# A two-attention transformer block with routed experts: weights handed over laid out, and the first copies of K sent ahead of Q

## The reference

```python
x = x + attn_a(layernorm(x))   # inside: layernorm, q/k/v with biases, 16 heads of 8,
                               # windows of 64 rows every 32, blended; wproj; residual;
                               # layernorm, MLP 128 -> 512 -> 128 with exact gelu
x = x + ffn(layernorm(x))      # router Wr (8 experts), top 2 of the softmax, renormalised;
                               # expert e: silu(x W1[e].T) W2[e].T
x = x + attn_b(layernorm(x))   # one head of 128, windows of 128 rows every 64, averaged
x = x + ffn(layernorm(x))      # the same experts again
```

## Time and profile before

| | |
|---|---|
| median of 3 runs | 584.41 us (582.85 to 586.38) |
| span of the profiled execution | 580.7 us |
| the profiled execution's own device time | not shown |
| PE busy | 483.9 us (83%) |
| DVE busy | 306.7 us (53%) |
| ACT busy | 243.7 us (42%) |
| POOL busy | 247.1 us (43%) |
| granted PE clock, mean | 0.891 |

### The profile page before, as it was taken

One profiled execution on the slowest core, in us unless ns is written; L12 is line 12 of the kernel. 1 busy time (PEld: TensorE's weight loads), 2 busy tenths in 40 slices (PEclk: granted clock), 3 DMA queues, 4 the chain that ended last, 5 costly groups with the idle time before them and its releaser, 6 DMA issues.

```text
span 580.7 us, 12462 instructions
## 1 busy us (share of the span) xinstructions
PE 483.9 (83%) x4005; PEld 383.5 (66%) x4027; DVE 306.7 (53%) x1012; ACT 243.7 (42%) x507; POOL 247.1 (43%) x229
## 2 busy tenths in 40 slices
PE   1879999999989999888799999907997499999960
PEld 0546776768666887585797787705777388787750
DVE  5676496858876898445740110055867743010116
ACT  7735566574547443604223232315764033232330
POOL 7143363335332655540547443520217536643450
PEclk9959899999989996968679999956999579999995
DMA  7882293985669183010022310040001222331007
GB/s 241 247 164 44 62 165 90 138 157 76 131 95 174 25 156 57 14 52 19 29 70 70 99 47 23 35 145 1 1 2 48 61 61 61 94 80 31 25 24 217
DMA packets 66593, 48.35 MB, mean 83 GB/s; under 512 B 7861, under 2 KB 60615, under 8 KB 66534
## 3 DMA queue, kind: packets, MB, share of 16 engines
q1 hardware_dynamic: 61430, 36.99, 31.0%
q0 software_dynamic: 5104, 10.57, 5.2%
HBM read 16.14 MB, written 27.59 MB: 75 GB/s over the span
## 4 chain that ended last, share of the span: by engine, by line
PE 67%; DVE 12%; issue 7%; SPq 5%; POOL 3%; DMA 3%; ACT 2%; DVEq 0%; POOLq 0%
PE PS L806 13%; PE PS L651 9%; PE PS L790 7%; PE PS L792 4%; SPq L303 4%; PE PS L638 3%; PE PS L791 3%; PE PS L613 3%; PE PS L701 3%; PE PS L554 2%; PE PS L661 2%; POOL XS L494 2%; PE PS L595 2%; PE PS L622 2%; PE PS L632 2%
## 5 line engine op out<-in xcount | busy, mean ns | idle before, releaser
L506 POOL DMA_INDIRECT YY<-W2R,ID x78 | 76.8, 985 | 84.0 <-ACT W2R L1263 65.4
L450 POOL TENSOR_TENSOR R<-NM,I64B 128x1024 bf16<-128x1024 f32 x32 | 61.6, 1924 | 109.1 <-DVE NM L1425 104.1
L1255 ACT ACTIVATE W2R<-PS 128x512 f32<-128x512 f32 x78 | 46.6, 597 | 121.2 <-PE PS L792 121.2
L806 PE MATMUL PS<-WB,W2R 128*128 x624 | 90.9, 291 | 0.1
L790 PE MATMUL PS<-QKM,WA 128*128 128x128 bf16 x312 | 73.2, 236 | 10.5 <-issue 4.3
L806 PEld LDWEIGHTS PS<-WB,W2R 128*128 128x128 f32 x624 | 78.1, 197 | 2.4 <-issue 0.3
L494 POOL DMA_INDIRECT XS<-W1R,SLOT x64 | 63.6, 994 | 37.0 <-DVE SLOT L1551 20.0
L1698 DVE COPY QKM<-PS 128x1024 bf16<-128x1024 bf16 (+1 forms) x20 | 13.5, 677 | 123.2 <-PE PS L769 123.2
L792 PE MATMUL PS<-QKM,WA 128*128 128x128 bf16 x312 | 73.2, 236 | 0.0
L791 PE MATMUL PS<-QKM,WA 128*128 128x128 bf16 x312 | 71.1, 229 | 0.0
L651 PEld LDWEIGHTS PS<-VB,PF 128*128 128x128 f32 x512 | 62.8, 201 | 8.6 <-issue 8.6
(11 more groups left out here) (207 smaller groups left out, 875.7 us busy)
## 6 DMA issues: line engine op xcount, KB each, us to landing
XS<-CST SPq DMA_DIRECT2D x30, 520.0 KB, 10.1
QKM<-XS SPq DMA_DIRECT2D x78, 65.0 KB
QKM<-QK SPq DMA_DIRECT2D x64, 72.0 KB, 2.1
QKM<-YY SPq DMA_DIRECT2D x16, 256.0 KB, 5.0
W2R<-in_W POOLq DMA_DIRECT2D x1, 2048.0 KB, 11.2
YY<-W2R,ID POOLq DMA_INDIRECT x78, 2.2
XS<-CST SPq DMA_DIRECT2D x2, 585.0 KB, 10.8
XS<-W1R,SLOT POOLq DMA_INDIRECT x64, 2.4
```

The costliest lines, as they stand in the source:

```text
L450: nc.gpsimd.tensor_tensor(R[:, u % 2], NM[:, u % 2].unsqueeze(2).to_broadcast([P, NH, WIN]), I64B[:].unsqueeze(1).to_broadcast([P, NH, WIN ...
L506: pool.indirect_dma_start(out=YY[f], out_offset=to, in_=YS[n % NY][:, i, :], in_offset=None, bounds_check=NPAIRS - 1, oob_is_err=False) \
L806: last = mm(o, HF[n % 3][:, k, :], WB[:, e, k, :].rearrange("p o c -> p (o c)"), start=k == 0, stop=k == KF - 1)
L1255: fn(HF[n % 3], PS[:, n % 3, :].rearrange("p (k s) -> p k s", k=KF), ACT.Silu).then_inc(s["f_hf"], 1)
```

## The change

The host hands the weights over laid out, and 8 loads take the place of 28 (and of POOL's 2): x of block 0, CST, EARLY (the small columns, Wr transposed, wq and wk; 139 KB), MID (the other small matrices and the MLP; 896 KB), three rows, x of blocks 1 to 3, W1 transposed (128 rows of 16 KB) and W2 transposed, which lands in WB itself (128 rows of 16 KB). All are on SP's queue. The transposes of W1, W2 and Wr, their waits and their copies out of PSUM are gone. What is left of W1's preparation is the bf16 split, now from SBUF: ACT copies expert t at the end of unit t (units 0 to 7), DVE subtracts expert t - 1 at the end of its work in unit t (units 1 to 8). WRT is a part of EARLY. HF and YS get a tile of their own (HYS).

`place` now sends the four K copies first, for every block and half, and Q and K have semaphores of their own: `scores` waits for K alone, `scores_t` for Q.

At the start POOL zeroes SELB instead of VB, and VB only after XZ of block 0 is done; DVE's 16 casts into SELB are spread, four each, between the variance steps and behind XZ. Waits of PE on the copies of transposed weights are replaced by waits on the copies of QK or QF that used the same PSUM bank.

The diff, cut ("..." marks what is left out):

```diff
+def laid_out(x):
+    column = lambda *names: [x[n].reshape(-1, P).T for n in names]
...
+    return {"x": x["x"], "early": np.concatenate(early, axis=1), "mid": np.concatenate(mid, axis=1),
+            "rows": np.concatenate([x[n] for n in ("bproj", "b2", "bo_b")])[None],
+            "W1t": x["W1"][::-1].transpose(2, 0, 1).reshape(P, NE * DFF),
+            "W2t": x["W2"][::-1].reshape(NE, D, KF, P).transpose(3, 0, 2, 1).reshape(P, NE * DFF)}
...
+            load(EARLY[:], a["early"], "ld_early")
+            load(MID[:], a["mid"], "ld_mid")
+            load(ROWS[:].rearrange("o r d -> o (r d)"), a["rows"], "ld_rows")
             load(X[:, TB:NT, :], xv[:, TB:NT, :], "ld_x_rest")
+            load(W1R[:], a["W1t"], "ld_w1")
+            load(WB[:].rearrange("p e k d -> p (e k d)"), a["W2t"], "ld_w2")
...
-                for m in range(2):
+                for m in (1, 0):
                     for i in range(4):
                         rows = slice(32 * i, 32 * i + 32)
-                        sp.dma_start(QKM[rows, m, half, i], QK[rows, m, half]).then_inc(s[f"a_m{half}"], 16)
+                        sp.dma_start(QKM[rows, m, half, i], QK[rows, m, half]).then_inc(s[f"a_{'qk'[m]}{half}"], 16)
...
-            nc.gpsimd.memset(VBF[:], 0.0).then_inc(s["pool_consts"], 1)
+            nc.gpsimd.memset(SELB[:], 0.0).then_inc(s["sel_zero"], 1)
...
             rstd(1, "a", 2)
-            nc.gpsimd.memset(SELB[:], 0.0).then_inc(s["sel_zero"], 1)
+            pool.wait_ge(s["a_xz"], TB)
+            nc.gpsimd.memset(VBF[:], 0.0).then_inc(s["pool_consts"], 1)
             pool.wait_ge(s["ld_const"], 16)
-            pool.dma_start(W2R[:], a["W2"].rearrange("e d f -> d e f")).then_inc(s["ld_w2"], 16)
-            pool.dma_start(WRN[:], a["Wr"]).then_inc(s["ld_router"], 16)
...
-                    pe.wait_ge(s[f"a_m{h}"], 16 * 8 * (b + 1))
+                    pe.wait_ge(s[f"a_k{h}"], 16 * 4 * (b + 1))
...
+                if t % 4 == 0:
+                    pe.wait_ge(s[f"a_q{h}"], 16 * 4 * (b + 1))
                 pe.wait_ge(s["a_r"], u + 1)
...
-            for e in range(NE):
-                pe.wait_ge(s["a_sel"], min(e, 3) + 1)
-                if e >= 4:
-                    pe.wait_ge(s["wt_lo"], e - 3)
-                transpose_weights(e, e % 4)
...
+            def weights_hi(e):
+                act.wait_ge(s["ld_w1"], 16)
+                fn(WA[:, 0, e, :], W1R[:, DFF * e:DFF * e + DFF], ACT.Copy).then_inc(s["wt_hi"], 1)
...
-                for e, bank in W2_STEPS.get((c, t), ()):
-                    weights_hi(NE + e, bank)
+                if c == 0:
+                    weights_hi(t)
...
+            def weights_lo(e):
+                dve.wait_ge(s["wt_hi"], e + 1)
+                hi, lo = (WA[:, c, e, :] for c in range(2))
+                v.tensor_tensor(lo, W1R[:, DFF * e:DFF * e + DFF], hi, ALU.subtract).then_inc(s["wt_lo"], 1)
...
+                if c == 0 and t >= 1:
+                    weights_lo(t - 1)
+                if c == 1 and t == 0:
+                    weights_lo(NE - 1)
...
             dve.wait_ge(s["ld_x"], 16)
             input_variance(0)
-            input_second_variance(0)
-            input_normalised(0)
             dve.wait_ge(s["ld_const"], 16)
             dve.wait_ge(s["sel_zero"], 1)
+            selectors(0)
+            input_second_variance(0)
+            selectors(1)
+            input_normalised(0)
+            selectors(2)
+            selectors(3)
             for m in range(2):
                 split_qk(0, m)
-            for e in range(NE):
-                weights_lo(e)
             input_variance(1)
```

More of the change, by code:

```diff
@@ L119, in constants @@
     return np.concatenate([c[n] for n in COLS], axis=1)
+EARLY_COLS, MID_COLS = {}, {}
+for _cols, _names in ((EARLY_COLS, (("cols_a", 6), ("cols_b", 3), ("b1", FA), ("bv", 1), ("Wr", NE), ("wq", D), ("wk", D))),
+                      (MID_COLS, (("wv", D), ("wproj", D), ("Wo_b", D), ("Wq_b", D), ("Wk_b", D), ("Wv_b", D),
+                                  ("w1", DA), ("w2", DA)))):
+    for _n, _w in _names:
+        _cols[_n] = (sum(w for _, w in _cols.values()), _w)
+NEARLY, NMID = (sum(w for _, w in c.values()) for c in (EARLY_COLS, MID_COLS))
+def laid_out(x):
+    column = lambda *names: [x[n].reshape(-1, P).T for n in names]
+    early = column("ln1_g", "ln1_b", "ln2_g", "ln2_b", "bq", "bk", "bq_b", "bk_b", "bv_b", "b1", "bv")
+    early += [x["Wr"].T, x["wq"], x["wk"]]
+    mid = [x[n] for n in ("wv", "wproj", "Wo_b", "Wq_b", "Wk_b", "Wv_b", "w1")]
+    mid += [x["w2"].reshape(FA, P, D).transpose(1, 0, 2).reshape(P, DA)]
+    return {"x": x["x"], "early": np.concatenate(early, axis=1), "mid": np.concatenate(mid, axis=1),
+            "rows": np.concatenate([x[n] for n in ("bproj", "b2", "bo_b")])[None],
+            "W1t": x["W1"][::-1].transpose(2, 0, 1).reshape(P, NE * DFF),
+            "W2t": x["W2"][::-1].reshape(NE, D, KF, P).transpose(3, 0, 2, 1).reshape(P, NE * DFF)}
 class Steps:
@@ L172, in program, with early, mid @@
         ident = cst("ident")
[L174 to L178, removed]
-        ROWS = sb("ROWS", [1, 3, D])
[L180 to L184, removed]
+        EARLY, MID, BQS = sb("EARLY", [P, NEARLY]), sb("MID", [P, NMID]), sb("BQS", [P, 1])
+        def early(name):
+            o, w = EARLY_COLS[name]
+            return EARLY[:, o:o + w]
+        def mid(name):
+            o, w = MID_COLS[name]
+            return MID[:, o:o + w]
+        COLA, COLB, B1A, BVA, WRT, WQ, WK = (early(n) for n in EARLY_COLS)
+        WV, WP, WOB, WQB, WKB, WVB, W1A = (mid(n) for n in MID_COLS if n != "w2")
+        W2A = mid("w2").rearrange("p (k n) -> p k n", n=D)
+        ROWS = sb("ROWS", [1, 3, D])
+        W1R, HYS = sb("W1R", [P, NE * DFF]), sb("HYS", [P, 7 * 512])
         WA = sb("WA", [P, 2, NE, DFF], BF16)
@@ L540, in program @@
         POOL_CONSTS = 13
[L541 to L545, removed]
         @block.tensor
@@ L551, in _, with tr @@
             mm = nc.tensor.matmul
[L553 to L564, removed]
+            def tr(dst, src):
+                return nc.tensor.transpose(dst, src, ident)
             def x_t(b):
@@ L915, in beside @@
                     logits(0, 0)
-                if t == 5 and c == 0:
-                    pe.wait_ge(s["ld_router"], 16)
-                    pe.wait_ge(s["a_sel"], 14)
-                    tr(PS[:, 7, 0:NE], WRN[:], NE).then_inc(s["wr_ps"], 1)
                 if t == 6 and c >= 1:
@@ L1121, in placed @@
                     act.wait_ge(s["a_st"], 2 * (NU * (b - 1) + 4 * half + 4))
-                    act.wait_ge(s[f"a_m{half}"], 16 * 8 * b)
+                    act.wait_ge(s[f"a_k{half}"], 16 * 4 * b)
+                    act.wait_ge(s[f"a_q{half}"], 16 * 4 * b)
                 if n < 4:
@@ L1208, in beside @@
                     placed(c + 1, 0, 4, 5)
-                if t == 5 and c == 0:
-                    act.wait_ge(s["wr_ps"], 1)
-                    fn(WRT[:], PS[:, 7, 0:NE], ACT.Copy).then_inc(s["wr_ready"], 1)
                 if t == 6 and c >= 1:
@@ L1650, in beside, with selectors @@
                     input_variance(c + 2)
-            dve.wait_ge(s["ld_x"], 16)
-            input_variance(0)
-            input_second_variance(0)
-            input_normalised(0)
-            dve.wait_ge(s["ld_const"], 16)
-            dve.wait_ge(s["sel_zero"], 1)
-            for g in range(NG):
+                if c == 0 and t >= 1:
+                    weights_lo(t - 1)
+                if c == 1 and t == 0:
+                    weights_lo(NE - 1)
+            def selectors(g):
                 rows = slice(32 * g, 32 * g + 32)
@@ L1664, in _ @@
                         v.tensor_copy(o[:, :, PIECE_OF[m][i]], e[:, :, PIECE_OF[m][i]]).then_inc(s["sel_ready"], 1)
+            dve.wait_ge(s["ld_x"], 16)
+            input_variance(0)
+            dve.wait_ge(s["ld_const"], 16)
+            dve.wait_ge(s["sel_zero"], 1)
+            selectors(0)
[4 more added lines that the diff above has]
+            selectors(3)
             for m in range(2):
                 split_qk(0, m)
-            for e in range(NE):
-                weights_lo(e)
             input_variance(1)
@@ L1876 @@
     arrays, args = {}, {}
-    for name, given in INPUTS:
-        arr = np.ascontiguousarray(inputs[given])
-        arrays["in_" + name] = arr
+    given = laid_out({name: np.asarray(inputs[full]) for name, full in INPUTS})
+    for name, arr in given.items():
+        arrays["in_" + name] = np.ascontiguousarray(arr)
         args[name] = nc.dram_tensor("in_" + name, arr.shape, F32, kind="ExternalInput").ap()
```

86 lines of the change are left out of this document (24 added, 62 removed).

## The result

| | kernel before | changed kernel |
|---|---|---|
| median, runs taken side by side | 583.72 us (582.85 to 586.38, 4 runs) | 575.87 us (574.49 to 577.57, 4 runs) |
| ratio, 95% interval | | 0.9866 [0.9834, 0.9899] |
| profiled execution: span, own device time | 580.7 us, not shown | 575.7 us, 577.57 us |
| granted PE clock of the profiled execution, mean | 0.891 | 0.902 |

A forecast was written before the change was run, and what follows sets the result against it. Latencies bound the start; in the loop PE binds until about 72 us, then DVE until 88.64. Start -6.0, loop +0.6 and clock -0.5 gave -5.9 us against 584.41, so 578.5 us, range 572.5 to 583.

The forecast's parts named there:

- The start: Up to the first scores: earlier normalising, fewer SP loads and K copies first bring them from 31.85 to 25.8, 6.0 us gained.
- the half allowed: Block 0's start: of 1.5 us won at XZ only 1.0 kept, as POOL's later zeroings stand near DVE's split.
- the lower bound of 3.5: Start's least gain, 3.5 us, if selector casts are caught behind POOL and only SP's share is left.
- The third rival: Start: first K copies wait in SP's queue behind two 2 MB loads; scores 10 us later, 595 us; chance 0.04.
- W1's transposes at nothing: Start: removing W1's transposes from PE earns nothing by itself, since they lay in PE's wait before the first score.
- The subtractions on DVE: Loop: eight of 0.68 us, hidden except at unit 3 (+0.6) and units 7 and 8 (+1.4).
- The second rival: DVE and POOL block each other: exposed subtractions cost 2.31 us each or selector casts are caught; 581 to 583.5; chance 0.17.
- Units 11 and 13, -0.9: Loop: removing two experts' transposes from a PE that binds there saves 0.9 us.
- the fourth rival: Clock stays down until unit 4 or falls again in PE-bound units: +3 to +6, 581 to 584 us; chance 0.06.
- The clock at the start, -0.5: PE's half clock around the first scores: same fall expected, bounds -1.7 and +1.7, taken as -0.5 us.
- What lies around the span: Gap between the profiled span (580.7) and the median of the runs (584.41) of the kernel before, set at 3.7 us.
- Later stages should only move: After the last edits, from the last attention block on, stages should shift in time without changing.

The follow-up runs named there:

- r0: The changed kernel run again, unaltered; mean 575.98 us, median 576.58 us.
- r2: The changed kernel run once more, unaltered, in a later call; mean 576.43 us, median 576.82 us.
- e7: Changed kernel with eight transposes of the identity, results unused, filling PE's wait before the first scores; mean 575.25 us, median 575.85 us.
- e8: Kernel before with only K's copies sent ahead of Q's, with own semaphores; mean 581.34 us, median 583.61 us.
- e1: Changed kernel with DVE's eight subtractions moved to units 1, 2, 4, 5, 6, 10, 14 and 14; mean 574.70 us, median 575.36 us.
- e6: Changed kernel with DVE's subtractions moved (units 1, 2, 4, 5, 6, 10, 14, 14) and x's variance earlier (7 to 5, 15 to 14); mean 573.64 us.
- e9: Changed kernel with subtractions moved, variance earlier and PE's first wait filled with eight transposes; mean 572.79 us, median 572.33 us.
- e2: Changed kernel with PE's 32 transposes of W2 put back in their old units, results unused; mean 575.07 us, median 574.79 us.
- e3: Changed kernel with the four Q copies sent ahead of the four K copies again; mean 579.67 us, median 579.24 us.
- e4: Changed kernel with POOL's zeroings and DVE's selector casts in the order of before; mean 575.81 us, median 576.51 us.
- e10: Changed kernel with subtractions moved and variance brought forward, the same list run a second time; mean 573.47 us, median 573.50 us.
- e5: Changed kernel with each of DVE's eight subtractions done twice, the second results unused; mean 581.67 us, median 581.64 us.

## Why the prediction was right, and where it was off

**The whole: right in the parts, lucky in the number.** The profiles give a lead of 5.9 to 7.5 us at the first scores (6.0 forecast) and of 3.2 to 3.6 in unit 29 (changed, r0, r2): the loop gave back 2.5 to 4.1, where 0.6 less 0.5 of clock was forecast. By the means the gain is 3.4 ± 1.3 and not 5.9; that the first four runs came to 7.85 is luck.

**The start: mechanism right, size by two errors that cancel.** XZ ended at 9.7 as forecast, and the casts were caught where nothing waited for them. HL began at 15.61, inside C's zeroing, and lost a quarter of a microsecond (0.69 instead of 0.44), not the half allowed. SP was idle, the copies take 0.6 each, the fourth lands 2.0 after its issue begins. Forecast 25.8; 25.7 to 26.0 in the runs with slow selection, 24.4 to 24.9 in those of the changed kernel, r0 and e7 with quick. The prediction didn't know that the selection has two rates: SP's first copy could start at 20.3 us in the changed kernel and at 21.8 in r2, where 21.05 was forecast. And from there to the first scores both take 4.1 us, not 4.7: the issues from 24.79 to 29.63 that the prediction counts as eight are seven in the trace of before, the eighth begins at 29.67, and the 2.04 of landing count from there. (Nor does the lower bound of 3.5 follow from its own terms, which add up to 5.2 less "a little".) The third rival is dead: the loads ran at 400 GB/s in 10 to 20 us, where the earlier trace rows have 357, and had all but ended when K was wanted (131 GB/s in 19 to 20 us); K's copies landed in 2.0 us as before.

**W1's transposes at nothing: right for the sum as long as the copies are late, wrong as a statement on cover.** e8 shows that they and their splits hold the start at 30.7 when K alone is sped up. The prediction named the wait for the copies as the cover and did not ask what is late next once these go.

**The subtractions on DVE: right.** e1 wins back 1.9 us of distance by moving them, where the two exposed terms are 2.0 (0.6 and 1.4). From the first scores to XZ of block 2 all terms gave +1.5 (0.6, -0.3, -0.2, 1.4); measured 0.9 (r2) to 2.2 (r0); but these distances also hold half clock that no term has: between 45 and 77 us it is 3.4 us in before, 3.4 in r2, 6.8 in the changed kernel and r0. The second rival's price stayed away here: no new subtraction lasted over 0.69 us, as these rows of the changed kernel show (duration ns min/median/max):

```profile
L1324 DVE TENSOR_TENSOR WA<-W1R,WA x8: 680/688/693, 32.3 to 76.4; 128x512 bf16<-128x512 f32 x8
```

```profile
L454 POOL TENSOR_TENSOR R<-NM,I64B x32: 1891/1902/2408, 26.2 to 235.2; 128x1024 bf16<-128x1024 f32 x32
```

**Units 11 and 13, -0.9: wrong, and here the clock failed the sum.** Between XZ of block 2 and unit 16 the changed kernel is 0.7 to 1.6 us slower than before, not 0.9 faster. The term is there when the clock stays up: 39.0 and 38.9 us in e6 and e9, against 39.7 in before, e8 and e2, which have the transposes. With the clock at half in 80 to 87 it is 40.4 to 41.3. In units 4 to 6 the clock takes its share too: from unit 4 to unit 6 the changed kernel needs 15.4 us, r2 13.7, with 6.8 and 3.4 us at half. The prediction argued against a new fall in the loop by PE's nearly full load from 46 us on; the trace of before already had one under that load, at 65.2 us, and the prediction had itself forecast that PE would wait, and did not carry that to the clock. So the fourth rival came true in part: 1.5 to 2.4 us behind XZ of block 2 (40.4 to 41.3 against 38.9), and 1.7 more in units 4 to 6 where that fall is the longer one.

**The clock at the start, -0.5: not borne out.** The fall is shorter (10 us at half, before about 14), but the price of 1.7 us that stands behind this term does not show: e7 takes most of the fall away and reaches unit 4 no sooner.

**What lies around the span: wrong.** I set it at 3.7 us from the median; it is 577.57 - 575.7 = 1.9. Against the profiled execution itself the same sum gives 580.7 + 1.9 - 5.9 = 576.7, 0.9 from the changed kernel's.

**"Later stages should only move": wrong.** The lead is 7.5 us at the first scores, 5.6 at XZ of block 2, 4.9 at unit 16, 3.6 in units 22 to 29, 6.9 at unit 30, 1.3 at unit 31 and 5.0 at the end. The chain of the changed kernel around the last two:

```profile
217.11 2.80 DVE HZ L1346 x4
...
222.54 0.19 PE PS L738
...
225.21 3.56 PE PS L639 x16
...
233.19 0.81 PE PS L599 x6
```

The mechanism is the same, DVE ahead of PE: PE waits for the router's choice in unit 30, and then `weighted` takes 3.56 us at half clock where 1.9 is its full-clock time. Before has a stretch at half clock there too (0.80 in 215 to 240 us in both), but it begins in unit 29, and in its unit 30 the router's choice is there when PE comes to it. What decides where the clock falls was not tried.

## What to carry to other kernels

Removing work from the busiest engine pays only where its clock stays up and nothing else ends later: look for the second engine's unbroken chain, and put new work where that engine has idle time in brackets. Handing the weights over laid out paid here through what it freed ahead of the first scores, and only together with the new order of the copies; the PE transposes saved in the loop showed no worth. When times scatter by more than the effect, compare means of many runs, and compare milestones of the traces.

## What the runs showed that was not expected

- The granted clock can fall in a loop that keeps PE nearly full, and waits explain it only in part. All seven traces in which PE waits 0.94 to 1.47 us ahead of `weighted` in unit 9 (changed, r0, r2, e1, e3, e4, e7) have about 6.8 us at half, which begin 1.1 to 3.6 us after that wait; before, e8, e2, e6 and e9, without that wait, keep 1.00 in 77 to 90 us, although e2, e6 and e9 wait 1.30 to 1.34 us for XZ of block 2. But e10, the same list as e6, falls for 3.4 us behind its 1.34. And the fall behind 50 us does not need the wait of 0.85 us: e1, e6 and e9 have one of 3.4 us there, with no wait over 0.25 us in the 15 us before it, while e10 has none. In e6 (PE's timeline, then a stage):

```profile
49.10 1.95 PE L639 MATMUL PS<-VB,PF 128*128 128x36 f32 x16 [0.24 <-issue]
```

```profile
52.00:53.00 1.00, 1.00 (x7) 0.50 0.00 0
```

  What tells these cases apart stays open. The Trainium skill (TensorE: Matmul & The Clock Gate, HAM oscillation) tells of a matmul kernel whose clock falls in the wait for a transfer ahead of each tile; here the waits are for another engine, and some falls follow no wait.
- The time of before goes with its mean granted clock: 3.8 us less per 0.01 over 101 runs. The traces show that much of this lies late. In unit 29 the profiles of e8, changed, r0 and r2 are 2.0, 3.6, 3.2 and 3.4 us ahead of that of before, at the end 8.6, 5.0, 4.6 and 2.3. The stages of e8 and then of before:

```profile
200.00:240.00 40.00, 37.12 (x307) 0.96 0.44 83
240.00:300.00 60.00, 49.17 (x400) 0.86 0.16 43
```

```profile
200.00:240.00 40.00, 39.09 (x304) 0.87 0.45 82
240.00:300.00 60.00, 49.82 (x350) 0.74 0.13 36
```

  Why the clock differs there from run to run was not settled.
- Eight subtractions with two SBUF inputs ran unhindered, but three times POOL's R, begun 0.04 to 0.05 us behind one of them, took 2.40 us instead of 1.90; in e5 four subtractions begun under R took 2.39. In these rows the one that starts second waits. The Trainium skill (GPSIMD Engine Reference, Key points) says that POOL contends for the SBUF interfaces with DVE instructions that have two SBUF inputs; the rows agree, and add the price of either order: 0.5 us for POOL, 1.7 for DVE.
- The 2 MB loads in 16 KB rows ran at 400 GB/s over 10 to 20 us. The Trainium skill (DMA: Bandwidth & Descriptors, Where 436 GB/s comes from) has about 358 as a core's share of the memory and 435 as the ceiling of the ports; the trace lies between the two. Two stages of 1 us show 459 (17 to 19 us), but each holds only 28 such rows, so that figure is coarse.
